# Output steps in two halves on TensorE, six slots for turned expert layers, and a new order of steps

## What is computed

```python
xn = layernorm(x)                                  # over the last axis
# attention: 16 query heads, 4 key/value heads, head size 16, rope, causal
q, k, v = xn @ wq, xn @ wk, xn @ wv
o = softmax(mask(rope(q) @ rope(k).T / 4)) @ v     # per head; 4 query heads share a key head
attn = o @ wo
# experts: 8 of them, hidden size 64, the two best of each token
scores = xn @ router_w.T; top2 = softmax(top_k(scores, 2))
h = silu(xn @ w1[e]) * (xn @ w3[e])                # bf16 operands
ffn = sum over the two experts e of top2[e] * (h @ w2[e])
out = x + attn + ffn
```

## Time and profile before

| what | value |
|---|---|
| time, median of 3 runs | 290.76 us (290.53 to 291.65) |
| the profiled execution | 290.62 us |
| its span | 288.9 us |
| PE busy | 262.5 us, 2307 instructions |
| DVE busy | 227.5 us, 312 |
| ACT busy | 244.4 us, 518 |
| POOL busy | 125.8 us, 260 |
| mean granted TensorE clock | 0.994 |

### The profile page before, as it was taken

One profiled execution on the slowest core, in us unless ns is written; L12 is line 12 of the kernel. 1 busy time (PEld: TensorE's weight loads), 2 busy tenths in 40 slices (PEclk: granted clock), 3 DMA queues, 4 the chain that ended last, 5 costly groups with the idle time before them and its releaser, 6 DMA issues.

```text
span 288.9 us, 6905 instructions
## 1 busy us (share of the span) xinstructions
PE 262.5 (91%) x2307; PEld 115.8 (40%) x2307; DVE 227.5 (79%) x312; ACT 244.4 (85%) x518; POOL 125.8 (44%) x260
## 2 busy tenths in 40 slices
PE   0868599999999999999999998999999999999996
PEld 0534355434344233334343443445523233433454
DVE  3663978999999999998999999995799898033342
ACT  1589876988999999999999998986689989898941
POOL 8386657363458418951135335246005414035020
PEclk9999889999999999999999999999999999999999
DMA  7537074110307103407371001023000300131307
GB/s 238 168 74 138 14 125 110 40 20 2 75 1 111 23 0 77 109 15 120 86 172 41 2 3 37 3 57 73 1 3 16 97 3 0 41 72 19 75 18 166
DMA packets 49106, 17.67 MB, mean 61 GB/s; under 512 B 43120, under 2 KB 48560, under 8 KB 49072
## 3 DMA queue, kind: packets, MB, share of 16 engines
q1 hardware_dynamic: 48384, 16.43, 26.8%
q10 hardware_dynamic: 688, 0.79, 0.8%
HBM read 4.46 MB, written 2.10 MB: 23 GB/s over the span
## 4 chain that ended last, share of the span: by engine, by line
PE 64%; DVE 12%; issue 8%; ACT 6%; POOL 5%; DMA 4%; POOLq 0%; SPq 0%; ACTq 0%
PE ps L808 18%; PE ps L790 13%; DVE PM L657 11%; PE ps L775 10%; PE ps L749 6%; PE ps L827 4%; ACT PR L543 3%; PE ps L848 3%; DMA HT<-HB 3%; PE ps L817 2%; PE ps L767 2%; PE ps L846 2%; PE ps L739 2%; DMA STACKS<-MIXED 1%; PE ps L835 1%
## 5 line engine op out<-in xcount | busy, mean ns | idle before, releaser
L543 ACT ACTIVATE PR<-ps,SCALE 128x512 f32<-128x512 f32 (+1 forms) x320 | 182.5, 654 | 15.7 <-PE ps L790 13.5
L657 DVE TENSOR_REDUCE PM<-ps 128x8 f32<-128x1024 f32 x144 | 167.8, 1218 | 9.0 <-PE ps L775 7.7
L453 POOL TENSOR_SCALAR_AFFINE_SELECT PR<-PR 128x512 f32<-128x512 f32 x64 | 39.8, 635 | 94.7 <-ACT PR L543 94.7
L808 PE MATMUL ps<-PR,VA 128*32 128x512 f32 (+3 forms) x768 | 78.1, 495 | 0.5 <-ACT OA L550 0.5
L790 PE MATMUL ps<-STACKS 64*128 64x512 f16 (+3 forms) x384 | 75.2, 327 | 2.9 <-ACT PR L543 1.4
L775 PE MATMUL ps<-STACKS 64*128 64x128 f16 (+2 forms) x640 | 59.2, 263 | 5.4 <-DVE PM L657 3.7
L790 PEld LDWEIGHTS ps<-STACKS 64*128 64x128 f16 x384 | 24.3, 93 | 57.0 <-ACT PR L543 43.6
L775 PEld LDWEIGHTS ps<-STACKS 64*128 64x128 f16 x640 | 27.1, 95 | 36.7 <-issue 32.1
L468 POOL TENSOR_TENSOR HB<-MIXED,GATE 128x512 bf16<-128x512 f32 x16 | 16.5, 1043 | 30.0 <-DVE MIXED L711 29.6
L808 PEld LDWEIGHTS ps<-PR,VA 128*32 128x32 f32 x768 | 17.0, 108 | 25.9 <-issue 21.1
L749 PE MATMUL ps<-WP,XT 128*128 128x392 f32 x64 | 25.7, 536 | 1.6 <-ACT XT L489 1.6
(11 more groups left out here) (92 smaller groups left out, 234.0 us busy)
## 6 DMA issues: line engine op xcount, KB each, us to landing
X<-x SPq DMA_DIRECT2D x8, 256.0 KB, 6.3
out<-X SPq DMA_DIRECT2D x16, 128.0 KB, 1.9
MIXED<-w SPq DMA_DIRECT2D x3, 512.0 KB, 3.8
STACKS<-MT SPq DMA_DIRECT2D x64, 2.0 KB
WP<-w_proj ACTq DMA_DIRECT2D x1, 392.0 KB, 4.3
WO<-wo ACTq DMA_DIRECT2D x1, 256.0 KB, 6.2
STACKS<-MIXED SPq DMA_TRANSPOSE x16, 3.6
MT<-MPW SPq DMA_TRANSPOSE x16, 2.5
```

The source lines that it names most:

```text
L453: mask = g.affine_select(out=blk, in_=blk, compare_op=ALU.is_ge, fill=0.0, base=0, pattern=[[0, GRP], [1, P]], channel_multiplier=-1)
L543: a.activation(PR[:, k % RING, j, 0:width], bank(step)[:, 0:width], ACT.Exp, scale=SCALE[:]).then_inc(s_exp, 1)
L657: v_.tensor_reduce(spots, two_banks(step).rearrange("p h (a s n) -> p h a s n", a=2, n=P), AX.X, ALU.max).then_inc(m_max, 1)
L808: mm = t_.matmul(o_bank[VW * j:VW * (j + 1), CHUNK - width:CHUNK], VA[:, b * KVH + grp, kb, :], PR[:, n % RING, j, at:at + width], start=i ...
```

## The change

An output step on PE is cut in two. The new kind share (Y) does the four matmuls with W2 and leaves its bank open; output (y) adds the four with WO in the same bank, with nothing to wait for but the copied attention rows. The bank counts as filled by the share and as read when DVE has taken the output. The slots of HT are six, and the transposing DMA waits for the share that used the slot, not for the whole output. All five strings of the order are new; every letter occurs as often as before, Y apart.

```diff
--- before.py
+++ after.py
@@ -43,7 +43,7 @@
 SLABS = QH + KVH * PILE
 VW = 32
 RING = 3
-HELD = 4
+HELD = 6
 LN_EPS = 1e-5
 BIG = 1e30
 
@@ -111,35 +111,35 @@
 
 ORDER = dict(
     PE=(
-        "xpxxPjjjxxxjxxjjjjmmmmmxxxmmJmJmmJmxmxxmJmJxmmJmsxmJmssmssmssmssmsvssmssmvssmsvmssmJmsmssvsmsssmvmss"
-        "smvsmssmvsmssssmssmsvsmsmssvrrsssrsmvssmsmvsmssvmssmssmssvmsssmvsmssmvssmssmsvmsssmvsmssmsvssmsmssms"
-        "vmsssmvsssmvmssmssmsvsmssmsvmsssmvmssrrssmsvssmsssvsssvmsssvsmssrsvssmmssvssmmssvssmsvmsssmsmsvmsssm"
-        "vssmsssmssmsvmssvmsmssvssmmssvssmsmsvssmsmvsmssvmssrsrsssmsmsvmssvmssmvssessEssvvssrrmssmssmvsssmmss"
-        "seessmvvEaamsssmvmssseEseymsssmvssmvssmaEEssyssrerssyvssmmssvaaeEssyymssvmssmsvmsssmvssmmssvmsssmvms"
-        "ssmvssmsseessEEessvmssmvssvmssEEssevmassmvsrsmssmsvsmssymsssmvssmssmsssvssvavsssyaasessvssyssEEssvss"
-        "vssyasseessvssEEssvsaevsssyssyssrrssvssvssveavEEryaaayayyy"),
+        "xxpPjjxxjjxjxxxjjjmmmxmxxmJmmJxmxmJmJmmxJmxmJmssmssmssmxsmsvmssmsmsssmJmssmvssmmvssmJmmsssvmsssmvssm"
+        "smvsmssmvssmsssmssmsvmssmsvssmsrrssmvrssmsvmsssmvmsssmvsmsssmssmsvssmsmvsmsssmsvmsssmvsmssmvssmsmsvm"
+        "sssmvssmsmsssmvsmssvmssmvmsssmvsmssmssrrssmssmvmsssmvmsssmvssmsmssvmssmssrsvssvssvssmsmsssvsssmvsmss"
+        "msvssmsmssvssmvsmssmssmssmsvssmsmvsmssvmsssmvmsssmvssmssrssrmssvssmvmssmssvssEessvvssrrsmsssmvsmsssm"
+        "sseessmvvsmsamssEEsseeYayamssmvssmvmssvEsseeYEssyYErrssymssamvmsssmvsmssvmasmssvmsssmvsmssmsvmsssmvs"
+        "mssYYssyEssysseeevssvssmvmssvssmEsseaEEsssrvmsssmvsmssmsvmssmssmsvsmssmssvssYYssvessEayassvssvssyssv"
+        "sseEessvYssEyssvsseaeYassyssvssvEssEarrssvssYEssvssyYssvYavyYryYaaYyyaaYyy"),
     ACT=(
-        "xNxNxzzjllxxNNzzljjlxxNxjjNjNjjNllzzzxxzzxllJzzJJxxxJJlzxJlsxJssssssssssssssssssvJssssssssssvsssssss"
-        "ssssssssvsssslsssssssssvssslssssssssssssssssssssssssvssslsssssssssssslssssslssssssssvssslsssssssssss"
-        "ssssssssssssvsssssssssssssssssssssssssssvsssssssssssGsvsssssssessvssssssssssseesssvaasssssesesssssss"
-        "svsassesssssssaaesssssssssssssssssvssssssessseesssssssssesassssssssssvssssssssssssasssaassesssssssss"
-        "ssvassssesessssassesssssssssssevaaaaa"),
+        "xxNNNNNllxjxjzzzzxljlxjxNxNjjjNjlzzzxxlxzzzJJlxxzzJJlxxJJssssssxsssslssssJsslssvssJsssssslsssvssssss"
+        "sssssssssssvslsssssssvsssssssssssssssssssssssslssssvssssssssslssssslsssssssssssslsssvsssssssssssssss"
+        "sssssssssssvsssGsssssssssssssssssssssssssvsssssssssssssvssssssessvssssssssssseessssssasseevsaassssss"
+        "vseesssssssassssssassssssssssssssssvssssseeesssssssssssaessssssssssvssssssssssssssssaeassssssssssees"
+        "svssssssaeeassssssssassssssssssvaaaaa"),
     DVE=(
-        "nnzWzzpnPjjznjjjjjjmmmmmMmmmmmmmMmmmmMmmmmmMmmmmmmmmmmmmmMmmmmmmmrrbbrbmmmmmmmMmmmmmmmmmmmmmMmmmmmmm"
-        "mmmmrrMbbmgmmmrbmmmMmmmmMmmmmmmmmmMMmmmmmmmmrrbbmmmmmGeMErrbbmmmmmemeEmmmEeeymmmmEEyMrrbbeymmEyeymmm"
-        "mmmmmmmmmeMEEeemmmEEemmrbmmmymmmmMyyEeEyeeEEyeyrrbbeEErbyyyyy"),
+        "nzzWnpnPjjnzzjjjjjjmmmmmMmmmmmMmmmmmmmMmmmmMmmmmmmmmmmmmmMmmmmmmmmrrbmbrbmmmmmmMmmmmmmmmmmMmmmmmmmmm"
+        "mmmmmrMrbbmmmmmmMmmmmrbgmmmMmmMmmmmmmmmmMmmmmmmrrbbmmmmGeErrbbmmmmMeemmmEEeeymmmmMEeeyEErrbbymmmmmmm"
+        "mmmmmmmMyyEeeemmmEEEerbmmmmmmmmmMyyeEeeEEyyeeErrbEEybyrbyyyyy"),
     POOL=(
-        "nnnjjllnjjlljjRlljjMllqqMMlsssMqssssMsssssllqsssMlqssMslqqlqlssMslsMssMMMcccssssssMEsssssEEsEEMsssss"
-        "EMsEEEEsssMEEsssEEEE"),
+        "nnnjjllnjjlljjRlljjMllMqsMqlMssqlssssMssqlssslsssMqqlsqssMlqlMssMlssMssMccssscMssssssEMEEssssEEMssss"
+        "MEEssssMEEEEsssEEEEE"),
     SP=(
-        "kkkkkktkkututtuutkukktutkukktkkuctcctuuttuuwtuwwyytwwuwtwwyyutuywwwwwwyyywwyyyyyyyy"),
+        "kkkkkktutkkuttuukktutkukktkuktkuccctuttuutuwtuwwyytuwwwwtyuytuwwyyyywwwwwwwyyyyyyyy"),
 )
 KINDS = dict(W="largest", p="range", P="scales", n="moments", N="spread", R="deviations", z="norm", x="turned", j="project", J="projected", q="rotated", l="parts", k="stacks", m="maxima", M="rows",
              t="rows_turned", u="rows_placed", s="scores", v="product", r="untwisted", b="quotients", g="rank", G="weigh", c="cast", e="experts",
-             E="factors", w="hidden", a="flat", y="output")
+             E="factors", w="hidden", a="flat", Y="share", y="output")
 
 BANKS_V, BANKS_S = 4, 3
-FILLED_V = dict(project=1, maxima=2, untwisted=1, experts=1, factors=1, output=1)
+FILLED_V = dict(project=1, maxima=2, untwisted=1, experts=1, factors=1, share=1)
 FILLED_S = dict(turned=1, projected=1, scores=1, flat=1)
 
 
@@ -272,8 +272,8 @@
                   "o_taken"))
         (r_ps, r_rcp, o_norm, a_ps, a_sb) = map(sem, ("r_ps", "r_rcp", "o_norm", "a_ps", "a_sb"))
         (gstep, gdiff, gexp) = map(sem, ("gstep", "gdiff", "gexp"))
-        (up_ps, tanhed, silu, f_ps, hidden, gated, y_ps, y_ready, y_out) = map(
-            sem, ("up_ps", "tanhed", "silu", "f_ps", "hidden", "gated", "y_ps", "y_ready", "y_out"))
+        (up_ps, tanhed, silu, f_ps, hidden, gated, y_half, y_ps, y_ready, y_out) = map(
+            sem, ("up_ps", "tanhed", "silu", "f_ps", "hidden", "gated", "y_half", "y_ps", "y_ready", "y_out"))
 
         def after(eng, s, count):
 
@@ -290,7 +290,7 @@
 
 
         READ_OUT = dict(turned=xb_sb, project=v_taken, projected=v_spread, maxima=m_max, scores=s_exp, untwisted=o_norm,
-                        experts=silu, factors=hidden, flat=a_sb, output=y_ready)
+                        experts=silu, factors=hidden, flat=a_sb, share=y_ready)
 
         def bank_free(step, at=0):
             before = places[step][at][1]
@@ -323,7 +323,7 @@
                 elif kind == "hidden":
                     sp.wait_ge(gated, n + 1)
 
-                    after(sp, y_ps, n - HELD + 1)
+                    after(sp, y_half, n - HELD + 1)
                     sp.dma_start_transpose(HT[:, n % HELD], HB[:, n % 2]).then_inc(h_turned[n % 2], 16)
                 elif kind == "rows_placed":
                     b, c, grp = JOBS[n]
@@ -712,7 +712,7 @@
                 elif kind == "output":
 
                     dve.wait_ge(y_ps, n + 1)
-                    v_.tensor_tensor(X[:, n, :], bank(step)[:, 0:D], X[:, n, :], ALU.add).then_inc(y_ready, 1)
+                    v_.tensor_tensor(X[:, n, :], bank(("share", n))[:, 0:D], X[:, n, :], ALU.add).then_inc(y_ready, 1)
 
         @block.tensor
         def _(pe):
@@ -834,18 +834,24 @@
                     for k in range(KT):
                         mm = t_.transpose(bank(step)[:, k * P:(k + 1) * P], AO[:, n, k * P:(k + 1) * P], IDF[:])
                     mm.then_inc(a_ps, 1)
+                elif kind == "share":
+                    if n == 0:
+                        pe.wait_ge(w_cast, 3)
+
+                    bank_free(step)
+                    pe.wait_ge(h_turned[n % 2], 16 * (n // 2 + 1))
+                    for k in range(EF // P):
+                        mm = t_.matmul(bank(step)[:, 0:D], HT[:, n % HELD, k, :], W2[:, k, :], start=(k == 0), stop=False,
+                                       skip_group_check=True)
+                    mm.then_inc(y_half, 1)
                 elif kind == "output":
                     if n == 0:
-                        pe.wait_ge(w_cast, 3)
                         pe.wait_ge(wo_in, 16)
 
-                    bank_free(step)
                     pe.wait_ge(a_sb, n + 1)
-                    pe.wait_ge(h_turned[n % 2], 16 * (n // 2 + 1))
-                    for k in range(EF // P):
-                        t_.matmul(bank(step)[:, 0:D], HT[:, n % HELD, k, :], W2[:, k, :], start=(k == 0), stop=False)
                     for k in range(KT):
-                        mm = t_.matmul(bank(step)[:, 0:D], AT[:, n % 2, k, :], WO[:, k, :], start=False, stop=(k == KT - 1))
+                        mm = t_.matmul(bank(("share", n))[:, 0:D], AT[:, n % 2, k, :], WO[:, k, :], start=False, stop=(k == KT - 1),
+                                       skip_group_check=True)
                     mm.then_inc(y_ps, 1)
```

## The result

| | kernel before | kernel changed |
|---|---|---|
| median | 291.41 us | 292.57 us |
| ratio to before, 95% interval | | 1.0044, 1.0028 to 1.0060 |
| profiled execution, its span | 290.62 us, 288.9 us | 292.15 us, 290.4 us |
| TensorE, VectorE, ScalarE busy | 262.5, 227.5, 244.4 us | 264.5, 227.2, 244.7 us |

(The two medians are from runs made side by side. Before the prediction, only the runs with the median of 290.76 us were known. One of the eight runs of before took 468.88 us; the ratio leaves it out, the median of 291.41 has it in.)

A forecast was written before the change was run, and what follows sets the result against it. Bounds: VectorE's maxima in the front, VectorE and ScalarE in the middle, TensorE in the tail. From 290.62 us, +1.0 front, +0.5 middle, -0.5 given back, -0.4 turned layer, -0.2 tail: 291.0, by the median 291.2; range 288.0 to 293.6.

The forecast's parts named there:

- The front: Start of the kernel, up to the first maximum: reordered norms and projections make it +1.0 us late, bounds -1.5 and +2.0.
- The walk: New front order traced with step durations from the old timeline; third projection on TensorE at about 19.5 us.
- The middle: Up to score 192: maxima drawn ahead delay scores, +0.5 us, bounds -1.5 and +2.5; ScalarE's slack gives back 0.5.
- Rival A: Scores 96 to 160: maxima drawn ahead not paid by idle time, VectorE's delay carries through, 293.2 us; chance 0.28.
- Rival B: Front starts sooner (-1.0 us), middle 0, tail closes its gaps (-0.4 -1.1): 288.3 us; chance 0.26.
- The tail: After score 192: shares between scores give -0.2 us, bounds -3.0 and +1.5, beside -0.4 for the turned layer.
- the slots: Six HT slots for four, in the tail: the last output's wait for the turned layer goes, -0.4 us.
- the copied rows: Tail, tiles 12 and 14: copying turned attention rows leaves at most 0.1 us of wait each, taken as 0.
- Switches and pairs: TensorE: four more operand-height switches cost +0.4 us, two fewer groups of paired scores give -0.4 us, net nothing.
- a held bank: Bank left open between share and output can stop maxima: costed at 0, upper bound +1.5 us.
- Transfers: SP: waits of 1.7 us on TensorE's outputs are off the path; later stack transposes hidden by some 1 us.
- The signs: Trace checks: first maximum, score 0, score 96, VectorE's idle time, TensorE's busy share, waits on HT and output reads.

The follow-up runs named there:

- e3: Changed kernel with 24 unread identity transposes on TensorE in its wait for norm 2: ratio 0.9999 to the kernel before, 290.87 us.
- e1: Changed kernel with the old order of steps up to the first maximum: ratio 1.0024 to the kernel before, 291.68 us.
- f5: As e1, but TensorE's next 11 steps also in the old order, maxima 3 and 4 ahead of tile 8: ratio 1.0024, 291.75 us.
- g3: Changed kernel with idle transposes on TensorE, 24 ahead of tile 2, 8 ahead of tile 8, 6 ahead of maximum 2: ratio 0.9945, 290.00 us.
- e2: Kernel before with only the new order up to the first maximum: ratio 1.0102, 293.92 us.
- g2: Changed kernel with four HT slots in place of six: ratio 1.0042 to the kernel before, 292.52 us.
- f4: As f2 (split outputs), but four HT slots: ratio 1.0098 to the kernel before, 294.06 us.
- g1: Changed kernel with the output in one piece, at the place of its second half, six slots: ratio 1.0128 to the kernel before, 295.15 us.
- f3: As f2, but the output in one piece at the place of its second half, six slots: ratio 1.0209, 297.29 us.
- e4: Kernel before in its own order, output cut into share and output next to each other, four slots: ratio 1.0011, 291.15 us.
- g4: Kernel before with 6 idle transposes on TensorE ahead of each of maxima 2, 3 and 4: ratio 0.9969, 290.59 us.
- f2: Old order up to score 195, then the new order with split outputs and six slots: ratio 1.0109 to the kernel before, 294.26 us.

## Why the prediction was right and wrong

*The front, +1.0 predicted (bounds -1.5 and +2.0), 4.15 us measured at the first maximum, 2.9 at score 32.* This is the term that failed. The walk had the third projection on TensorE at 19.5 us; it came at 20.16. The mechanism, norms 2 and 3 behind two projections and the last moments, was right, and by e3 it costs some 0.6 us of the first maximum. But the walk took 1.3 to 1.6 us for every projection, those of a TensorE at full clock, across a wait of some 3 us that it had itself made. The clock fell to 0.50, and that costs the other 3.5 us (2.3 to 3.6 by the bounds under e3). It was a term missing from the sum, and from the bounds: the trace of before has the same fall at 34 to 38 us, and the stretch of 30.3 to 52.0 with its clock of 0.92 stood in front of me. So did the price: of the three projections from 10.77 us the first takes 2.77 us (10.77 to 13.54) and the last 1.3, though the clock column has 1.00 for that stretch. The Trainium skill (TensorE: Matmul & The Clock Gate, section Part 1: The HAM clock gate) says that the half rate is the default state and sustained activity releases it; the trace agrees, with 0.50 right after the wait of 3.15 us. Worked out with this, two projections of 2.75 us for 1.36 are 2.8 us, and the first maximum of VectorE would have been forecast at 34.2 (30.37 + 1.0 + 2.8); it came at 34.53:

```profile
34.53 2.36 DVE L657 TENSOR_REDUCE PM<-ps 128x8 f32<-128x1024 f32 x2 [0.57 <-PE ps L775]
```

*The front's end.* I let it end at the first maximum. The steps up to score 32 are part of it: e1 and f5 bring the first maximum to before's time within 0.9 and 0.05 us and are still 2.9 and 1.8 us late at score 32; the changed kernel goes from 4.15 to 2.90 there, g3 from 1.0 to -0.2. In the old order these steps hand a delay on (e2, 3.3 to 3.1).

*The middle, +0.5 - 0.5 predicted, 0.0 measured* (from +2.90 at score 32 to +2.95 at score 192; -0.01 to +0.12 in the six other traces of the new middle). That score 96 would come 1 to 2.5 us late, score 160 less and score 192 hardly was right: over the shift at score 32 they are +2.0, +1.2 and 0.0. On VectorE's own line maximum 20 is 2.6 us late, maximum 60 2.7 and maximum 70 2.4: the line stands still up to there, which fits the reason given, that the scores are late by the maxima drawn ahead of them. But its idle time was 3.46 us, not under 2.5.

*Rival A, 293.2 us.* The nearest to the measured time, and half right. Its heading, that VectorE's line carries a delay through, is what e2 shows (3.3 us at the first maximum, 3.1 at every score). But its place, the maxima drawn ahead between scores 96 and 160, is worth 2.0 us over the front's shift at score 96, and that is gone by score 192. What is carried is the front.

*Rival B, 288.3 us,* was wrong in its first half (-1.0 front) and right in its second: it gave the tail -1.5 in all, and -1.4 was measured.

*The tail, -0.2 - 0.4 predicted, -1.4 measured after score 192.* The 0.4 stood under the slots. The wait of L846 on HT<-HB is gone from the changed trace, as said, but equally so with four slots, and g2 and f4 show the slots worth nothing: it went because the order puts the last experts further ahead. The shares between other steps were put at -0.2; g1 and f3 give them 2.4 and 2.6 us in this order. I had written that the copied rows leave "at most 0.1 us of wait each"; in g1's last two pairs the step after the turning starts 0.45 us later than with a share between. Nearly half of that gain only makes good what the order without a split would lose: by g1, from score 192 to the end it is 1.2 us longer than before.

*Switches and pairs, 0.* No experiment parts them. The halves by themselves cost nothing measurable (e4), and a drain of 0.09 us for each of four more switches is below what can be seen. The upper bound of 1.5 us for maxima stopped by a held bank was not needed: in the changed kernel no maximum waits for an output's read (L715).

*Transfers.* SP's waits on TensorE's outputs are gone, off the path, as said. The stacks' later issue was not wholly hidden: maximum 20, the first that needs them, waits 0.43 us for them (59.15). That is small.

*The signs.* First maximum (L657) at 31 to 32 us: 34.53, wrong. Score 0 at 50 to 51: 52.73, wrong. Score 96 at 115.5 to 117: 119.40, wrong by the front's shift of 2.9. TensorE over 98% in the last 100 us: 96.6% (94.12 of 97.46). I had also said that the forecast was wrong if score 192 lay over 2 us off 178.2: at 180.16 it is 1.96 us off, and the steps behind it were wrong. That the total came within 1.4 us of the forecast is partly luck: a front that was 1.9 us too cheap met a tail that was 0.8 too dear, and neither error was foreseen.

## What to carry to other kernels

Wherever an edit makes TensorE wait, or leaves it sparse, look at the granted clock of the stretches behind that wait in the trace at hand, and price the matmuls there at both levels; the fall can cost more than the lateness that brings it on (here 3.5 us behind 0.6 at the first maximum). Matmuls of no use in an unavoidable wait are a cheap cure to try. A step cut in two gains nothing by itself; it gains where its free half can stand in the place of a wait, so count those places, and judge an order piece by piece. Cut the pieces where both orders have done the same steps: at other places a shift of one step mixes time lost with work done early, and a gain can be read into the next piece that isn't there.

## What the hardware showed that was not expected

- One and the same wait can leave the clock or lose it. Up to the first maximum g4 has before's steps. TensorE waits 2.00 us for the same norm in before and 2.01 in g4, and some two microseconds later the clock is at 1.00 in one and at 0.50 in the other (timeline and stretch of before, then of g4):

```profile
22.09 0.93 PE L739 MATMUL ps<-IDF,MIXED 128*128 128x128 f32 x4 [2.00 <-ACT MIXED L506]
24.00:26.00 2.00, 1.51 (x6) 0.76 (x5) 0.95 (x3) 2.00 (x8) 1.89 (x5) 1.00 0.19 43
```

```profile
21.63 0.93 PE L739 MATMUL ps<-IDF,MIXED 128*128 128x128 f32 x4 [2.01 <-ACT MIXED L506]
24.00:26.00 2.00, 2.00 (x4) 1.00 (x4) 0.95 (x3) 1.97 (x8) 1.53 (x4) 0.50 0.47 75
```

- The waits of 3.15 us in the changed kernel, 2.34 us after some sparse maxima (e1) and 1.99 us (f2) were each followed by 0.50 to 0.64. Before loses the clock even without a wait of that size, at 34 to 38 us, among maxima with some 0.7 us between them.
- 24 plain f32 transposes took 2.78 us and kept the clock at 1.00 over the wait of e3; 6 to 8 were enough at the other places.
- Making the sum of a bank in two steps, one right behind the other, costs nothing measurable (e4: 1.0011, 0.9994 to 1.0029). What it costs to leave it open while other banks are filled and read, as the changed kernel does, no run shows by itself.
- What stays open: g4's profiled execution is 0.6 us late from score 0 on although its timed runs are 0.3% faster. It is one of the two of its 12 runs at a mean clock of 0.994, by the fall after 22 us shown above, so its trace doesn't show where the gain of the others lies beyond the clock from 34 to 38 us. Open too is which steps between the first maximum and score 32 cost or give back time.
